# Set-up of the projection weights handed from VectorE to GpSimd, and a new order of the first four pairs, in a fused attention and slot-mixing kernel

## The reference, cut to what matters

```python
xn = layernorm(x)
q = tanh(xn @ W_charge.T + b_charge)
shell = xn @ W_shell.T + b_shell
proj = (shell / norm(shell)) @ omega.T + rff_bias
phi_s = concat([cos(proj), sin(proj)]) * scale
phi = (q ** [0..4] outer phi_s) @ W_combine.T
attn = softmax(causal(phi @ phi.T * T / temp))
x = x + (attn @ (xn @ W_v.T + b_v)) @ W_out.T + b_out
xm = layernorm(x)
h = gelu([xm, slot_mean] @ w1.T + b1)
alpha = top8_softmax(h @ w2.T + b2)
slots = gru(alpha.T @ xm / alpha.sum, S0)
out = x + (alpha @ (slots @ wv.T + bv)) @ wo.T + bo
```

## Time and profile before

| | us |
|---|---|
| median of 3 runs (lowest, highest) | 689.96 (689.7, 691.14) |
| the profiled execution's own time | 689.95 |
| its span, first to last instruction | 688.1 |
| PE busy (share) | 672.6 (98%) |
| DVE busy | 605.0 (88%) |
| ACT busy | 514.3 (75%) |
| POOL busy | 386.9 (56%) |

### The profile page before, as it was taken

One profiled execution on the slowest core, in us unless ns is written; L12 is line 12 of the kernel. 1 busy time (PEld: TensorE's weight loads), 2 busy tenths in 40 slices (PEclk: granted clock), 3 DMA queues, 4 the chain that ended last, 5 costly groups with the idle time before them and its releaser, 6 DMA issues.

```text
span 688.1 us, 15845 instructions
## 1 busy us (share of the span) xinstructions
PE 672.6 (98%) x4626; PEld 541.6 (79%) x4626; DVE 605.0 (88%) x2001; ACT 514.3 (75%) x1478; POOL 386.9 (56%) x818
## 2 busy tenths in 40 slices
PE   8999999999899999999999999999999999999996
PEld 5867878787697887879798787979878787978774
DVE  6688998797989898998989899898989989899984
ACT  4979889777596896959698695968879596875461
POOL 3727867362665747376565737556583756655200
PEclk9999999999999999999999999999999999999999
DMA  8343020204233050323215042421504242121004
GB/s 237 109 153 93 1 63 1 63 2 137 49 103 81 20 158 11 122 63 118 67 38 148 2 125 61 123 63 57 130 1 134 53 123 62 63 62 63 1 32 152
DMA packets 49115, 54.11 MB, mean 79 GB/s; under 512 B 6212, under 2 KB 40582, under 8 KB 49030
## 3 DMA queue, kind: packets, MB, share of 16 engines
q1 hardware_dynamic: 48260, 52.57, 27.7%
q10 hardware_dynamic: 770, 0.53, 0.3%
HBM read 20.58 MB, written 16.78 MB: 54 GB/s over the span
## 4 chain that ended last, share of the span: by engine, by line
PE 87%; SPq 3%; DVE 3%; ACT 2%; issue 2%; POOL 2%; DMA 1%; DVEq 0%; ACTq 0%; POOLq 0%
PE ps L321 17%; PE ps L349 16%; PE ps L443 15%; PE ps L476 6%; PE ps L546 6%; PE ps L415 6%; PE ps L531 4%; PE ps L641 4%; PE ps L488 2%; SPq L1717 2%; PE ps L392 2%; PE ps L617 2%; PE ps L398 2%; PE ps L395 2%; PE ps L308 1%
## 5 line engine op out<-in xcount | busy, mean ns | idle before, releaser
L241 POOL TENSOR_TENSOR Z<-Z,QB 128x512 f32<-128x512 f32 x60 | 77.4, 1290 | 80.6 <-ACT Z L834 78.8
L779 ACT ACTIVATE xn<-X,rs 128x255 f32<-128x255 f32 x128 | 66.4, 599 | 72.0 <-POOL rs L1563 72.0
L349 PE MATMUL ps<-W1h,xh 128*128 128x354 f32 x256 | 88.6, 346 | 0.0
L443 PE MATMUL ps<-Vh,Eh 128*128 128x256 f32 x320 | 88.6, 304 | 0.0
L349 PE MATMUL ps<-W1h,xl 128*128 128x354 f32 x256 | 83.2, 325 | 0.6 <-DVE xl L1039 0.5
L349 PE MATMUL ps<-W1l,xh 128*128 128x354 f32 x256 | 83.0, 324 | 0.0
L443 PE MATMUL ps<-Vl,Eh 128*128 128x256 f32 x320 | 80.9, 280 | 0.0
L845 ACT ACTIVATE E<-ps,nmax 128x128 f32<-128x128 f32 (+3 forms) x128 | 67.9, 536 | 9.7 <-DVE nmax L1095 9.5
L1103 DVE TENSOR_TENSOR El<-ps,Eh 128x128 fp32r<-128x128 f32 (+3 forms) x128 | 61.7, 483 | 13.2 <-ACT Eh L855 11.7
L1046 DVE TENSOR_TENSOR Vl<-ps,Vh 128x256 fp32r<-128x256 f32 x128 | 53.5, 419 | 21.7 <-ACT Vh L804 19.3
L268 POOL TENSOR_SCALAR xm<-X,rs 128x256 f32<-128x256 f32 x120 | 68.0, 581 | 2.2 <-POOL rs L1572 1.0
(11 more groups left out here) (245 smaller groups left out, 1961.9 us busy)
## 6 DMA issues: line engine op xcount, KB each, us to landing
X<-in_x SPq DMA_DIRECT2D x32, 512.0 KB, 4.4
xmT<-Z SPq DMA_DIRECT2D x120, 128.0 KB, 2.3
out_x<-X SPq DMA_DIRECT2D x30, 512.0 KB, 3.7
out_x<-X SPq DMA_DIRECT2D x4, 256.0 KB, 2.5
X<-in_gru_whhT SPq DMA_DIRECT2D x1, 768.0 KB
wih<-in_gru_wihT SPq DMA_DIRECT2D x1, 768.0 KB, 6.1
X<-in_W_v ACTq DMA_DIRECT2D x1, 256.0 KB, 4.5
...
```

The lines of the kernel that those rows point to most:

```text
L241: e.tensor_tensor(Z[:, i + 1, :], Z[:, i, :], QB[:, :], ALU.mult).then_inc(s["zm"], 1)
L349: ins = e.matmul(p[:, 0:FEATS], x[:, d, c, t * 128:t * 128 + 128], w[:, c, :], start=j == 0, stop=j == 5)
L443: ins = e.matmul(p[:, 0:D], w[:, r % 2, j * 128:j * 128 + 128], v[:, (2 * k + d) % 4, j, :], start=z == 0, stop=z == len(parts) - 1)
L779: ins = e.activation(xn[:, d, t, 0:D - 1], X[:, b % NX, t, 0:D - 1], ACT.Identity, bias=rs[:, d, 2, t:t + 1], scale=rs[:, d, 1, t:t + 1])
```

## The change

`values_setup` and `shell_setup` go from DVE's list to POOL's, ahead of `ln_scale(0, 0)`. The first batch's `ln_norm(0, 0)` is done for token tiles 0 and 1 by ACT and for 2 and 3 by DVE (`norm_setup`), with a new semaphore `ln_half` for which `xn_t` of batch 0 waits. `first_warm` has four products. The lists of the head are written in another order on PE, ACT, DVE and POOL; SP's list, the loop and the end are as before. All line numbers behind the changed places move by 2 to 10.

```diff
@@ tensor
                 e.wait_ge(s["ln_n"], b + 1)
+                if b == 0:
+                    e.wait_ge(s["ln_half"], 2)
...
                 e.wait_ge(s["warm"], 1)
-                for _ in range(6):
+                for _ in range(4):
...
-            proj(0, 0, 0); proj(0, 0, 1); xn_t(0, 1, 0); xn_t(0, 1, 1); proj(0, 0, 2); proj(0, 0, 3)
+            proj(0, 0, 0); xn_t(0, 1, 0); proj(0, 0, 1); xn_t(0, 1, 1); proj(0, 0, 2); proj(0, 0, 3)
...
-            slot_setup(); gates_setup(); states_setup(0); states_setup(1); states_setup(2); q_t(0)
+            slot_setup(); q_t(0); gates_setup(); states_setup(0); states_setup(1); states_setup(2)
...
-            xm_t(2, 1, 1); e_t(3, 4); gx_rz(1); q_t(4); hidden(2, 1); z_t(4); logits(3, 2); route(2); gx_n(1)
-            rt_t(2); values(3, 3); e_t(3, 5); al_t(1); values(3, 4); values(3, 5); e_t(3, 6); e_t(3, 7)
-            slot_v(1); values(3, 6); values(3, 7); phi(4); gather(2); logits(4, 0); out_mm(1, 0); gi_t(2)
+            xm_t(2, 1, 0); xm_t(2, 1, 1); q_t(4); gx_rz(1); hidden(2, 1); e_t(3, 4); logits(3, 2); route(2)
+            gx_n(1); rt_t(2); values(3, 3); values(3, 4); e_t(3, 5); z_t(4); values(3, 5); e_t(3, 6)
+            e_t(3, 7); al_t(1); slot_v(1); values(3, 6); values(3, 7); phi(4); gather(2); logits(4, 0)
+            out_mm(1, 0); gi_t(2)
@@ scalar
-                for t in range(4):
+                for t in range(4 if b else 2):
                     ins = e.activation(xn[:, d, t, 0:D - 1], X[:, b % NX, t, 0:D - 1], ACT.Identity,
                                        bias=rs[:, d, 2, t:t + 1], scale=rs[:, d, 1, t:t + 1])
...
@@ vector
+            def norm_setup():
+                e.wait_ge(s["ln_b"], 1)
+                for t in (2, 3):
+                    e.tensor_scalar(xn[:, 0, t, 0:D - 1], X[:, 0, t, 0:D - 1], rs[:, 0, 1, t:t + 1],
+                                    rs[:, 0, 2, t:t + 1], ALU.mult, ALU.add).then_inc(s["ln_half"], 1)
...
-            clear_setup(); ln_stats(0, 0, 0); ln_stats(0, 0, 1); scale_a_setup(); values_setup()
-            shell_setup(); ln_stats(0, 1, 0); ln_stats(0, 1, 1); scale_b_setup(); weights_high()
-            weights_low(0); weights_low(1); xn_low(0, 0, 0); ln_stats(1, 0, 0); xn_low(0, 0, 1)
+            clear_setup(); ln_stats(0, 0, 0); ln_stats(0, 0, 1); scale_a_setup(); ln_stats(0, 1, 0)
+            ln_stats(0, 1, 1); norm_setup(); scale_b_setup(); weights_high(); weights_low(0); weights_low(1)
+            xn_low(0, 0, 0); xn_low(0, 0, 1); ln_stats(1, 0, 0); bias_setup(); ln_stats(1, 0, 1)
...
@@ gpsimd
-            scales_setup(); ln_scale(0, 0); ln_scale(0, 1); attention_setup(); ln_scale(1, 0); temper_setup()
+            scales_setup(); values_setup(); shell_setup(); ln_scale(0, 0); ln_scale(0, 1); attention_setup()
...
```

More of the change, by code:

```diff
@@ L724, in _ @@
-            q_t(3); values(2, 3); e_t(2, 4); xm_t(1, 1, 0); gx_rz(0); xm_t(1, 1, 1); xn_t(4, 0, 1)
-            values(2, 4); hidden(1, 1); e_t(2, 5); z_t(3); logits(2, 2); route(1); gx_n(0); values(2, 5)
-            al_t(0); e_t(2, 6); rt_t(1); proj(4, 0, 0); values(2, 6); phi(3); xn_t(4, 1, 0); e_t(2, 7)
-            proj(4, 0, 1); proj(4, 0, 2); logits(3, 0); xn_t(4, 1, 1); values(2, 7); proj(4, 0, 3)
-            proj(4, 1, 0); e_t(3, 0); proj(4, 1, 1); proj(4, 1, 2); xm_t(2, 0, 0); e_t(3, 1); proj(4, 1, 3)
@@ new lines, in _ @@
+            xn_t(1, 1, 0); states_setup(3); xn_t(1, 1, 1); states_setup(4); proj(1, 0, 0); proj(1, 0, 1)
+            z_t(0); proj(1, 0, 2); states_setup(5); proj(1, 0, 3); phi(0); proj(1, 1, 0); logits(0, 0)
+            proj(1, 1, 1); proj(1, 1, 2); e_t(0, 0); proj(1, 1, 3); e_t(0, 1); logits(0, 1); e_t(0, 2)
+            values(0, 0); e_t(0, 3); values(0, 1); logits(0, 2); e_t(0, 4); values(0, 2); q_t(1); e_t(0, 5)
+            values(0, 3); values(0, 4); z_t(1); xn_t(2, 0, 0); xn_t(2, 0, 1); e_t(0, 6); values(0, 5)
@@ new lines, in _ @@
+            e_t(1, 5); values(1, 4); z_t(2); hidden(0, 1); e_t(1, 6); xn_t(3, 1, 0); values(1, 5); route(0)
+            proj(3, 0, 0); rt_t(0); values(1, 6); proj(3, 0, 1); xn_t(3, 1, 1); phi(2); e_t(1, 7)
+            proj(3, 0, 2); proj(3, 0, 3); logits(2, 0); xn_t(4, 0, 0); values(1, 7); proj(3, 1, 0); e_t(2, 0)
+            xm_t(1, 0, 0); proj(3, 1, 1); values(2, 0); logits(2, 1); e_t(2, 1); proj(3, 1, 2); xm_t(1, 0, 1)
+            e_t(2, 2); proj(3, 1, 3); gather(0); e_t(2, 3); hidden(1, 0); values(2, 1); e_t(2, 4); gi_t(0)
@@ new lines, in _ @@
+            values(2, 2); gx_rz(0); q_t(3); xn_t(4, 0, 1); values(2, 3); xm_t(1, 1, 0); xm_t(1, 1, 1)
+            values(2, 4); hidden(1, 1); z_t(3); e_t(2, 5); logits(2, 2); route(1); al_t(0); gx_n(0)
+            values(2, 5); e_t(2, 6); rt_t(1); proj(4, 0, 0); values(2, 6); phi(3); xn_t(4, 1, 0); e_t(2, 7)
+            proj(4, 0, 1); proj(4, 0, 2); proj(4, 0, 3); logits(3, 0); xn_t(4, 1, 1); values(2, 7)
+            proj(4, 1, 0); e_t(3, 0); proj(4, 1, 1); xm_t(2, 0, 0); proj(4, 1, 2); proj(4, 1, 3)
@@ new lines, in _ @@
+            v_high(3, 1, 0); xm_copy(1, 0, 0); v_high(3, 1, 1); ln_norm(4, 1); probs_t(2, 1); probs_t(2, 2)
+            v_high(3, 1, 2); v_high(3, 1, 3); xm_copy(1, 0, 1); expo(2, 4); expo(2, 5); gelu(1, 0)
+            probs_t(2, 3); gi_copy(0); charge(3); probs_t(2, 4); sine(3); q_copy(3); xm_copy(1, 1, 0)
+            xm_copy(1, 1, 1); xn_high(4, 0, 1); gelu(1, 1); probs_t(2, 5); rz_tanh(0); z_copy(3); expo(2, 6)
+            rt_out(1); probs_t(2, 6); al_copy(0); v_high(4, 0, 0); expo(2, 7); probs_t(2, 7); v_high(4, 0, 1)
@@ new lines, in _ @@
+            inverse(1, 3); v_low(3, 0, 0); top(0, 1, 0); top(0, 1, 1); attended(1, 6); lm_stats(1, 5)
+            shift(0, 0); lm_stats(1, 6); v_low(3, 0, 1); qk_full(2); shift(0, 1); v_low(3, 0, 2)
+            probs_low(1, 7); xn_low(3, 1, 1); row_max(2, 0); row_max(2, 1); row_max(2, 2); row_max(2, 3)
+            chosen(0, 0); attended(1, 7); v_low(3, 0, 3); inverse(2, 0); weight_sum(0, 0); xn_low(4, 0, 0)
+            lm_stats(1, 7); probs_low(2, 0); weight_sum(0, 1); v_low(3, 1, 0); xm_low(1, 0, 0); chosen(0, 1)
@@ new lines, in _ @@
+            lm_stats(2, 4); row_max(2, 6); row_max(2, 7); probs_low(2, 5); candidate(0); probs_low(2, 6)
+            attended(2, 5); top(1, 0, 0); top(1, 0, 1); top(1, 1, 0); top(1, 1, 1); inverse(2, 3)
+            v_low(4, 0, 0); attended(2, 6); qk_full(3); lm_stats(2, 5); shift(1, 0); lm_stats(2, 6)
+            shift(1, 1); weight_sum(1, 0); probs_low(2, 7); v_low(4, 0, 1); chosen(1, 0); v_low(4, 0, 2)
+            row_max(3, 0); row_max(3, 1); v_low(4, 0, 3); xn_low(4, 1, 0); row_max(3, 2); xn_low(4, 1, 1)
@@ L1491, in _ @@
+            attended(3, 1); lm_stats(3, 1); quarter_turn(4); xm_low(2, 1, 0); xm_low(2, 1, 1); gates(1)
+            attended(3, 2); lm_stats(3, 2); inverse(3, 2); row_max(3, 6); row_max(3, 7); probs_low(3, 4)
+            candidate(1); top(2, 0, 0); top(2, 0, 1); top(2, 1, 0); top(2, 1, 1); probs_low(3, 5); shift(2, 0)
+            shift(2, 1); new_slots(1); attended(3, 3); weight_sum(2, 0); attended(3, 4); attended(3, 5)
             probs_low(3, 6); probs_low(3, 7); chosen(2, 0); inverse(3, 3)
```

214 lines of the change are left out of this document (93 added, 121 removed).

## The result

| | before | after |
|---|---|---|
| median of 6 runs (lowest, highest), us | 689.83 (689.01, 691.14) | 694.85 (694.61, 695.18) |
| ratio, 95% interval | | 1.0070 (1.0058 to 1.0083) |
| span of the profiled execution | 688.1 | 692.9 |
| PE busy | 672.6 | 674.0 |
| mean granted clock | 0.998 (profiled execution) | 0.989 to 0.992 (all runs) |

A forecast was written before the change was run, and what follows sets the result against it. It took PE, busy 98% of the span, plus its waits in head and end as the bound. The terms +0.2 + 0 + 0 - 1.7 gave -1.5 us against 689.95, so 688.4 us, range 686.7 to 691.2.

The forecast's parts named there:

- step 3: Head: four constant products end at about 7.6, PE then waits until 10.25; worth 0 in PE time.
- step 1: Head: shifts on POOL take about 2.2 us, weight products start at 10.25 in place of 9.34, +0.9 us.
- What bounds the kernel: Whole kernel: PE's work plus its waits in head and end; the change is worth when PE enters the loop.
- Step 2: Head: first norm shared by ACT and DVE, done at 12.55, covered by 1.6 us, worth 0.
- Step 4: First projection: wait before 16.57 shrinks by 0.6, xn_t(0, 1, 0) costs +0.9; PE 1.2 us late at proj(0, 0, 2).
- Step 5: Head up to the first phi: waiting for slot loads and later gaps absorb most of the delay, leaving +0.2 us (0 to +0.8).
- Step 6: 43 to 150 us: 0 change, ends -0.7 and +0.8 us.
- Step 7: 150 to 190 us: earlier angle steps end the sine's wait, slot_v(1) and phi(4) come earlier, -1.7 us (0 to -3).
- Rival B: Head: PE's clock falls in the gap before the weight products, +3.2 us there, total 691.5 us; chance 0.13.

The follow-up runs named there:

- pooladd4: The changed kernel, four constant products, with each shift on POOL written as times one plus the negated last column: 694.68 us, ratio 1.0069.
- actnorm: The changed kernel with the shifts back on DVE, six constant products and the first norm wholly on ACT: 688.44 us, ratio 0.9980.
- dve6: The changed kernel with the shifts back on DVE and six constant products: 688.10 us, ratio 0.9971 against the kernel before.
- bpool6: The kernel before with the shifts alone moved to POOL, six constant products, old lists: 695.4 us, ratio 1.0077.
- warm9b: The changed kernel with nine constant products in place of four, second measurement: 691.13 us, ratio 1.0024 against the kernel before.
- angle4: The kernel before with DVE's remainder(4), mirror(4) and quarter_turn(4) moved earlier, behind turns(4): ratio 1.0010.
- qt4: The kernel before with one exchange on PE's list, q_t(4) ahead of gx_rz(1): ratio 1.0000.
- seg4q: The kernel before with the new order from xm_t(2, 1, 0) on, but q_t(4) back behind gx_rz(1): 688.75 us, ratio 0.9973.

## Why the prediction was wrong

It had 688.4 us (686.7 to 691.2), most likely with an absorbed head and a shorter late stretch; 694.85 was measured. The step that failed by most is step 3: the pause that it leaves in front of the weight products stood in the sum at nothing, and it brought the clock down (at 12.4, just after the pause), which cost 3.2 us (`proj(0, 0, 0)` at 19.87, and at 16.66 without the pause). Second is the price in step 1, +0.9 in the sum and +2.0 measured. In the profiled executions the sum was off by 6.3 us (-1.5 against +4.8): 3.2 by the clock, 1.1 by the shifts, 0.6 that was not absorbed, 0.8 between 43 and 150 us, 0.7 behind `phi(4)`, less 0.1 in the late stretch. Point by point:

- **What bounds the kernel**: held. The loop takes what it took, and the change is worth the moment at which PE enters it, 4.1 us later at `phi(4)`. Some 0.7 more is lost between there and the last product; I have no cause for it. The profiled executions of the other kernels are longer there too, by 0.1 to 0.9 us.
- **Step 1, shifts on POOL**: right in its mechanism, wrong in its price. The start at the landing of b_v, DVE's gain of nothing (it waits 1.09 us for x) and the power queued behind were as forecast. The price was not: 0.93 us in place of 0.58, so +2.0 us at the weight products in place of +0.9. My row showed a pair of operations where the shift is a lone one, and I took its size as what counts. "Same operation at the same size" was wrong in its first half. The range stopped at the row's value, since I took the far end from the other side (DVE's 1.2 us). The right price alone would not have saved the forecast: pooladd4, with shifts of 0.57 us, takes 694.68.
- **The Trainium skill's remark on this step**: POOL's 0.93 us against DVE's 0.31 is not "roughly line-rate". The Trainium skill, "GPSIMD Engine Reference", section "Engine selection", has it so for one input; its advice to put such work on VectorE agrees with the trace, its remark doesn't, for this form.
- **Step 2, shared norm**: held as to its worth: actnorm equals dve6.
- **Step 3, constant products and the pause, worth 0 in PE time**: the step that failed. PE's work did not change, its clock did, by 3.2 us; the step named this as a rival and left it out of the sum. It is the pause that counts more than the two removed products: with six products and the late shifts bpool6 lost as much. The removal made the pause longer, and so did the clock's early rise: four products end at 7.16 and not 7.6, because the clock rose at 5.5 us here and not at 6.8.
- **Step 4 and the head's order**: dve6 starts `proj(0, 0, 2)` 0.4 us later than before (18.97 against 18.59), against the +0.3 that step 4 leaves without the late shifts, and reaches the first `phi` 0.3 us earlier than before, against my +0.2. Held.
- **Step 5, absorption by the slot loads**: 0.7 us on the old lists (bpool6), where I had taken 1.0, and next to nothing on the new ones. The slack I read off belonged to the old order. POOL's `slot_setup` ends at 30.07 in place of 26.1: it stands behind `ln_scale(1, 0)`, which waits for statistics of a DVE that is itself late. The work I counted on as fixed moves with the delay. In warm9b it ends at 27.06 and PE's slot products start at 27.96, 1.95 later than in dve6, with no loss of clock in it.
- **Step 6, 43 to 150 us**: +0.8 (5.1 to 5.9), at my upper end.
- **Step 7, 150 to 190 us**: the size held (-1.8 in the change, -2.6 in dve6, against -1.7 with an end of -3), the cause only by half. I named the angle as what the sine waits for. My own row had named PE's L321, the transposes of q. Angle and transposes end within 0.2 us of each other there, but only the transposes held the table load: moving the angle alone did nothing for it (angle4), moving `q_t(4)` alone brought it forward (qt4). And an earlier sine is only part of the gain (seg4q).
- **Rival B** is what happened, at 0.13 in place of most of the chance. It gave 691.5; with the true price of the shifts (+1.1), nothing absorbed (+0.6) and 3.2 instead of 2.6 for the clock it gives 693.8, and step 6 brings it to 694.6. That this comes so near to 694.85 is partly luck: it is 0.4 too high at the first `phi` (5.5 against 5.1) and has nothing for the 0.7 lost behind `phi(4)`. Its point of decision, a pause near 2.65 us, was right: 2.61 dropped the clock in five runs of five. The evidence for it, the end of the program, showed 0.53 after a pause of 2.7 us. I set against it only that no such pause stood in the middle, which is no evidence. And I took 2.65 us for the most the pause could be, when both of its ends were uncertain and lay on the same side.
